# Split queries and keys copied from their tile to the matmul stacks in 18 SBUF transfers per unit, without the scratch tensor in DRAM

## The reference

```
g = (x * ac_w + ac_b) * x;  g = clip(g, 0, 6)                 # x is _gn(x)
qkv = einsum('bchw,dc->bdhw', g, qkv_w)                       # split into q, k, v: 16 heads x 8 channels
attn = softmax(einsum('wnqd,wnkd->wnqk', q, k) * scale)       # inside each 8x8 window
out = einsum('bchw,dc->bdhw', einsum('wnqk,wnkd->wnqd', attn, v), proj_w) + proj_b
x = x + L0(_gn(x))
x = x + conv3x3(_gn(x), W) + bias
```

## Time and profile before

| what | value |
|---|---|
| median of three runs | 1202.87 us |
| the profiled execution | 1207.08 us, of it a span of 1205.3 us |
| TensorE matmul busy | 1015.8 us (84%) |
| VectorE busy | 983.1 us (82%) |
| ScalarE busy | 791.3 us (66%) |
| GpSimd busy | 503.8 us (42%) |
| mean granted TensorE clock | 0.947 |
| DMA packets, bytes | 114917, 140.59 MB |

### The profile page before, as it was taken

One profiled execution on the slowest core, in us unless ns is written; L12 is line 12 of the kernel. 1 busy time (PEld: TensorE's weight loads), 2 busy tenths in 40 slices (PEclk: granted clock), 3 DMA queues, 4 the chain that ended last, 5 costly groups with the idle time before them and its releaser, 6 DMA issues.

```text
span 1205.3 us, 52690 instructions
## 1 busy us (share of the span) xinstructions
PE 1015.8 (84%) x23011; PEld 582.6 (48%) x23011; DVE 983.1 (82%) x1312; ACT 791.3 (66%) x1327; POOL 503.8 (42%) x469
## 2 busy tenths in 40 slices
PE   0388999999999985998853899999999999779996
PEld 0155565556555652433321555556655655334442
DVE  6786888889888754899986788888988976379996
ACT  1257787778778774655532688878887877556663
POOL 5214454445444433233343245545454544404335
PEclk9879999999999997999986899999999999879998
DMA  8234444444444420133343454444444444001112
GB/s 307 84 118 125 136 138 138 136 137 128 135 142 135 142 64 1 44 129 108 105 157 122 123 150 139 136 137 138 144 132 148 134 142 126 4 1 53 70 70 88
DMA packets 114917, 140.59 MB, mean 117 GB/s; under 512 B 25088, under 2 KB 91008, under 8 KB 113664
## 3 DMA queue, kind: packets, MB, share of 16 engines
q1 hardware_dynamic: 114688, 137.23, 36.3%
HBM read 67.96 MB, written 67.11 MB: 112 GB/s over the span
## 4 chain that ended last, share of the span: by engine, by line
PE 63%; DVE 18%; issue 8%; DMA 4%; ACT 3%; SPq 2%; POOL 2%; POOLq 0%; DVEq 0%; ACTq 0%
PE ps L918 11%; PE ps L899 11%; PE ps L926 9%; PE ps L885 8%; PE ps L995 6%; PE ps L853 5%; DVE work L760 5%; PE ps L854 5%; PE ps L855 5%; DVE work L756 4%; PE ps L872 4%; DVE st L610 1%; SPq L288 1%; DVE work L738 1%; DMA q_bd<-stack_scratch 1%
## 5 line engine op out<-in xcount | busy, mean ns | idle before, releaser
L654 DVE TENSOR_REDUCE m_all<-ps 128x16 f32<-128x1024 f32 x256 | 313.5, 1225 | 114.9 <-PE ps L885 114.3
L370 POOL TENSOR_SCALAR work<-work 128x256 f32<-128x256 f32 x128 | 108.6, 849 | 401.2 <-DVE work L647 352.4
L885 PEld LDWEIGHTS ps<-k_pl,q_bd 48*64 48x64 f16 x8192 | 90.4, 111 | 174.5 <-issue 126.9
L448 ACT ACTIVATE late_probs<-ps,ws 128x1024 f32<-128x1024 f32 x128 | 142.8, 1116 | 44.6 <-PE ps L899 42.8
L853 PE MATMUL ps<-work,c_hi 128*128 128x512 f16 x384 | 148.3, 386 | 27.7 <-DVE work L760 27.7
L899 PE MATMUL ps<-q_bd,k_pl 128*64 128x256 f16 x2048 | 163.8, 282 | 7.5 <-ACT work L448 4.0
L885 PE MATMUL ps<-k_pl,q_bd 48*64 48x64 f16 x8192 | 118.6, 198 | 57.3 <-issue 39.4
L536 ACT CAST work<-work 128x512 f16<-128x512 f32 (+1 forms) x128 | 79.0, 622 | 115.8 <-DVE work L756 107.9
L448 ACT ACTIVATE work<-ps,ws 128x1024 f32<-128x1024 f32 x128 | 141.7, 1107 | 13.1 <-PE ps L899 11.5
L854 PE MATMUL ps<-work,c_lo 128*128 128x512 f16 x384 | 148.0, 385 | 0.0
L855 PE MATMUL ps<-work,c_hi 128*128 128x512 f16 x384 | 147.4, 384 | 0.0
(11 more groups left out here) (126 smaller groups left out, 1894.1 us busy)
## 6 DMA issues: line engine op xcount, KB each, us to landing
stack_scratch<-work SPq DMA_DIRECT2D x128, 256.0 KB, 2.4
q_bd<-stack_scratch SPq DMA_DIRECT2D x256, 96.0 KB
k_pl<-stack_scratch SPq DMA_DIRECT2D x128, 192.0 KB, 3.5
stack_scratch<-work SPq DMA_DIRECT2D x128, 128.0 KB, 2.5
out_dram<-work SPq DMA_DIRECT2D x32, 512.0 KB, 2.9
img<-in_x_dram SPq DMA_DIRECT2D x8, 1024.0 KB, 13.4
img<-in_x_dram SPq DMA_DIRECT2D x16, 512.0 KB, 4.3
q_bd<-m_pair SPq DMA_DIRECT2D x256, 8.0 KB
```

The source lines that it names most:

```text
L370: g.tensor_scalar(near[h], near[h], -2.0, None, ALU.add).then_inc(less_done, 1)
L448: a.activation(probs[h][:, p % 2, :], ps[:, ST_B:ST_B + 2, :].rearrange("p w t -> p (w t)"), ACT.Exp, scale=ws[:, R_EXP:R_EXP + 1]).then_i ...
L654: v.tensor_reduce(m_all[:, 0, :, p], ps[:, S_B:S_B + 2, :].rearrange("p r (a k) -> p (r a) k", k=WIN), AX.X, ALU.max).then_inc(max_done, 1)
L885: mm = t_.matmul(ps[64 * w:64 * w + 64, S_B + r, at:at + WIN], q_bd[rows, md, r, g, j, tok], k_pl[rows, md, g, tok], start=True, stop=True)
```

## The change

The scratch tensor in DRAM, `write`, `q_sent` and `k_sent` go. SyncE copies each part of `qk` straight to every third partition of the stacks: for the keys 3 parts times 2 halves, 6 transfers of 64 rows of 1 KB; for the queries 3 parts times 4 quarters, 12 transfers of 32 rows of 1 KB. Keys now go before queries, and the maxima stand ahead of both. ScalarE's next rounding of `qk` waits until the transfers have landed in the stacks (`k_in`, `q_in`) where it waited for the write to DRAM (`k_sent`, `q_sent`). So that a part's rows are neighbours in `qk`, the columns of the query and key weights are put in another order once, at the start: three copies where there was one, on ScalarE and on VectorE.

```diff
-        q_sent = sem("q_sent", 32); k_sent = sem("k_sent", 32)
-        q_in = sem("q_in", 64); k_in = sem("k_in", 32)
+        q_in = sem("q_in", 16 * HR * HJ * PARTS); k_in = sem("k_in", 16 * HR * PARTS)
...
                 def queries_in(d, md):
-                    after(sp, q_sent, d)
+                    after(sp, q_lo_done, d)
                     after(sp, st_done, d - BUFS)
                     after(sp, q_in, d - 1)
-                    q_rows = stackd[md, 0].rearrange("(r g j d) s t -> r j (d s) g t", r=HR, g=HG, j=HJ)
-                    for r in range(HR):
-                        for j in range(HJ):
-                            at = 64 * r + HROWS * j
-                            sp.dma_start(q_bd[at:at + HROWS, md, r, :, j, :], q_rows[r, j]).then_inc(q_in, 16)
+                    for s, part in enumerate((0, 1, 1)):
+                        for r in range(HR):
+                            for j in range(HJ):
+                                at, ch = 64 * r + HROWS * j, 64 * r + 32 * j
+                                sp.dma_start(q_bd[at + s:at + HROWS:PARTS, md, r, :, j, :], qk[ch:ch + 32, part, :]).then_inc(q_in, 16)
 
                 def keys_in(d, md):
-                    after(sp, k_sent, d)
+                    after(sp, k_lo_done, d)
                     after(sp, st_done, d - BUFS)
                     after(sp, k_in, d - 1)
-                    k_rows = stackd[md, 1].rearrange("(r g a) s t -> r (a s) g t", r=HR, g=HG)
-                    for r in range(HR):
-                        sp.dma_start(k_pl[64 * r:64 * r + ROWS, md, :, :], k_rows[r]).then_inc(k_in, 16)
+                    for s, part in enumerate((2, 3, 2)):
+                        for r in range(HR):
+                            sp.dma_start(k_pl[64 * r + s:64 * r + ROWS:PARTS, md, :, :], qk[64 * r:64 * r + 64, part, :]).then_inc(k_in, 16)
...
+                    if live(1):
+                        maxima(n + 1, (m + 1) % BUFS)
                     if live(3):
+                        keys_in(n + 3, (m + 3) % BUFS)
                         queries_in(n + 3, (m + 3) % BUFS)
-                        keys_in(n + 3, (m + 3) % BUFS)
-                    if live(2):
-                        maxima(n + 2, (m + 2) % BUFS)
-                    if live(4):
-                        after(sp, q_in, n + 1)
-                        write(0, n + 4, (m + 4) % BUFS, q_lo_done, q_sent)
-                        after(sp, k_in, n + 1)
-                        write(1, n + 4, (m + 4) % BUFS, k_lo_done, k_sent)
...
-            a.copy(w_hi[:, :, :], ps[:, 0, 0:3 * P].rearrange("p (t d) -> p t d", t=3)).then_inc(act_step, 1)
+            for k in range(3):
+                a.copy(by_column(w_hi, k), by_head(k)).then_inc(act_step, 1)
...
                         after(act, k_done, n + 3)
-                        after(act, k_sent, n + 2)
+                        after(act, k_in, n + 2)
                         a.copy(qk[:, 2, :], ps[:, GB, :]).then_inc(k_hi_done, 1)
...
                         after(act, q_done, n + 3)
-                        after(act, q_sent, n + 2)
+                        after(act, q_in, n + 2)
                         a.copy(qk[:, 1, :], ps[:, GA, :]).then_inc(q_hi_done, 1)
```

More of the change, by code:

```diff
@@ L61, in build @@
 def build(nc, x, ac_w, ac_b, qkv_w, proj_w, proj_b, conv_w, conv_b, out):
-    stackd = nc.dram_tensor("stack_scratch", [BUFS, 2, P, PARTS, UT], F16, kind="Internal").ap()
     ctx = ExitStack()
@@ L188, in pixels, with by_head, by_column @@
             return (u // ACROSS) * WS, (u % ACROSS) * UCOL
+        def by_head(k):
+            cols = ps[:, 0, k * P:k * P + P]
+            return cols if k == 2 else cols.rearrange("p (r g j d) -> p r j d g", r=HR, g=HG, j=HJ)
+        def by_column(w, k):
+            return w[:, k, :] if k == 2 else w[:, k, :].rearrange("p (r j d g) -> p r j d g", r=HR, j=HJ, g=HG)
         block = ctx.enter_context(nc.Block())
@@ L599, in weak_weights @@
                 for j in range(MATS // 4):
-                    dve.wait_ge(act_step, 3 + j)
+                    dve.wait_ge(act_step, 5 + j)
                     v.tensor_tensor(c_lo[:, 4 * j:4 * j + 4, :], ps[:, 2 + j, :].rearrange("p (t d) -> p t d", d=P),
@@ L606, in _ @@
                 if i == 2:
-                    dve.wait_ge(act_step, 1)
-                    link(v.tensor_tensor(w_lo[:, :, :], ps[:, 0, 0:3 * P].rearrange("p (t d) -> p t d", d=P), w_hi[:, :, :], ALU.subtract))
+                    dve.wait_ge(act_step, 3)
+                    for k in range(3):
+                        link(v.tensor_tensor(by_column(w_lo, k), by_head(k), by_column(w_hi, k), ALU.subtract))
                 dve.wait_ge(x_in[i * LOADS // UNITS], 16)
@@ L855, in three @@
                 return t_.matmul(o, lhs_hi, rhs_lo, start=False, stop=last)
-            pe.wait_ge(act_step, 2)
+            pe.wait_ge(act_step, 4)
             norm_mean(0)
```

## The result

The changed kernel takes 1541.93 us (median of four runs, 1540.04 to 1554.21), the kernel before 1201.18 beside it: a ratio of 1.285, 95% interval 1.276 to 1.294. It is slower, as forecast, but by 341 us where 210 were forecast: 1542 against 1413, just inside the upper edge of the range (1280 to 1545), next to the 1545 of the rival "heavier than that".

What follows compares the result with a forecast made beforehand. TensorE bounds the kernel at 12.0 us a unit; the new ring takes 9.5 issues + 1.7 stalls + 1.7 landing + 2.5 rest = 15.4, with starts 105 us per image, 210 in all: 1413 us, range 1280 to 1545.

Steps and rivals of the forecast that it cites:

- heavier than that: Rival, chance 0.17: all eighteen issues at 0.635 us, TensorE's clock lower, lap (a unit's period) 17.7 us, total 1545.
- What bounds the kernel now: Attention loop runs at TensorE's pace, 12.0 us a unit; SyncE's queue has thin cover, some landings late.
- The ring: SyncE's transfers, landing, ScalarE's rounding and exponential, TensorE, st_done, next keys: one lap 15.4 us against 12.0.
- The price of a query issue: Each SyncE query transfer holds the queue 0.53 us; the step trusted least, 0.1 us being 95 us in all.
- The two ends: Issue prices taken as limits: 0.615 us for SyncE's maxima transfers, 0.40 for its reads from DRAM.
- The key issue: Each of six 64-row key transfers on SyncE priced at the upper end, 0.615 us.
- Landing and way back: After the last query issue: 1.7 us to land, 2.5 through ScalarE and TensorE until the next keys.
- Stalls: SyncE's queue at times held longer for the same work: 1.7 us per 18 issues.
- How many laps, and the start: 28 longer laps per image, 95 us, plus 10 us together for the stage's start and last units.
- Bytes and weights: Halved DMA traffic costed at nothing; extra weight copies on ScalarE at the start cost nothing.
- Cheap issues: Rival, chance 0.12: SyncE's transfers cost 0.40 us like reads, lap 12.3 us, 27 us more, total 1230.
- the faster side: Rival, chance 0.04: an issue costs 0.33 us or less, TensorE binds at 11.2, late landings go, total 1155.

Runs made afterwards that it cites:

- e8: Kernel before with three DRAM writes a unit instead of four, second copies of queries and keys merged into one transfer: 1221.70 us (1.010).
- e6: Kernel before with SyncE's four writes to DRAM put ahead of the maxima transfers: 1317.20 us (1.093).
- e12: Changed kernel with two qk tiles, TensorE's last transposed scores ahead of the waiting scores, and ten transfers (keys, third query part) on GpSimd: 1170.88 us (0.973).
- e2: Changed kernel with two qk tiles in turn, so ScalarE's rounding waits for the landing of the unit before the last: 1471.01 us (1.221).
- e3: Changed kernel with two qk tiles, and TensorE's last part of the transposed scores ahead of the scores that wait for transfers: 1468.43 us (1.218).
- e1_price: Kernel before with eleven bursts of 12 transfers, one shape each, after its last output; only issue times read: new forms 0.713 and 0.637 us.
- e5_short_rows: Changed kernel with all 18 transfers a unit but each row cut from 1 KB to 128 bytes: 1527.71 us (1.263).
- e9_pool_keys: Changed kernel with two qk tiles, TensorE's last transposed scores ahead of the waiting scores, and keys issued by GpSimd at its iteration's end: 1548.97 us (1.280).

## Why the prediction was right, and where it was short

**What bounds the kernel now: right.** TensorE set the pace of the kernel before (93% and 94% busy), and the transfers had little slack: `e8` shows a time 12 us longer when the tiles' way waits 0.9 us more a unit, and `e6` shows that the maxima beside them had 2 to 3 us. That the way of the tiles itself cost time before fits `e12` (a mean lap of 11.4 us against 12.2 in the first image, while TensorE's waits for these landings fell from 24.0 to 8.2 us over both images), but no run changes that alone.

**The ring: right, and seen whole.** Landing, rounding and exponential, last part of the transposed scores, `st_done`, keys: each handover stands in the rows of after, and the maxima are hidden (SyncE waits from 302.60 to 304.23, 1.6 us; 1.2 forecast). `e2` and `e3` add that the queue itself comes next, 22 issues and 15.2 us, only 1.5 us under the ring. The prediction gave the ring's ties and its issues as one sum; the experiments part them: with both ties cut, 74 of the 341 us come back, and the other 267 stay with the length of the queue.

**The price of a query issue: the term most undersized.** It was put at 0.53 us, between the maxima's 0.615 and the reads' 0.40, because the transfer fills whole rows of partitions as the reads do. It costs 0.713, above both ends. From first query issue to last that is 7.94 against 5.83 us, 2.1 us a lap. The two ends were not bounds. The prediction put the gap between maxima and reads down to the two sides' shapes and then took off 0.085 for full rows. What parts the two rows is that both sides lie in SBUF: at 32 rows on both sides an issue still costs 0.633 (`e1_price`), and bytes do not count (`e5_short_rows`). The last 0.08, from 0.633 to 0.713, goes with 8 destination partitions (L335 and L344 of `e1_price`); why they cost more stays open. The key issue, 0.615 forecast, costs 0.636.

**Landing and way back: 0.3 us short each.** 2.07 for 1.75, and 2.79 for 2.45, the latter because L898 took 1.07 us at a granted clock of 0.56 where 0.63 was the row at full clock. The effect was named only in the heavy rival.

**Stalls: 1.3 us too long.** The mean lap from the maxima is 17.1 us, 0.4 over the undisturbed 16.69, where 1.7 was forecast from two units of before. So the lap: 15.4 + 2.1 + 0.2 + 0.3 + 0.3 - 1.3 = 17.0.

**How many laps, and the start: short.** The period holds for all 30 units from the second on, (610.7 - 95.2 - 1.9) / 30 = 17.1 and (1366.6 - 854.2 - 1.9) / 30 = 17.0:

```profile
L290 SPq DMA_DIRECT2D q_bd<-m_pair x124: 503/586/1777, 95.2 to 610.7; - x124
...
L290 SPq DMA_DIRECT2D q_bd<-m_pair x124: 502/586/1189, 854.2 to 1366.6; - x124
```

The forecast had 28 laps and 10 us of start per image; the second unit's maxima come 95.2 - 80.1 = 15.1 us later. 2 x (30 x 5.1 + 15) = 336, the 333 us between the two spans. First scores begin at 63.24 where 62 was forecast.

**Bytes and weights: right.** Halved traffic is worth nothing by itself, and the weight copies cost nothing: VectorE's statistics end at 34.1 us in the profile after.

**The prediction's own sums.** Three do not come out as written, none of them large. The lower end of the range, 1280, is called an issue of 0.45; by its own 95 us for each 0.1 us that is about 1310, and 1280 belongs to an issue of 0.42. The first scores add up to 51.1 + 10.0 + 1.7 = 62.8, not 62. And the maxima's bytes move 1.15 to 1.33 us after the issue starts, not 1.2 to 1.4.

**Luck.** The mechanism was right, but the central sum was 131 us short of 341. It lay inside the range only because the upper end was drawn at the heavy rival's 1545, 3 us above the result, and that rival's terms were off in both directions: its issues too short (10.8 us a lap against 3.89 + 7.94 = 11.8), its laps too few (28 against 30), its stalls too long (2.2 against 0.4).

**The rivals.** Cheap issues and the faster side are out by the price. Behind the latter stood the Trainium skill's rule that the issue time is usually small relative to the DMA itself ("DMA: Bandwidth & Descriptors", "Issuing engines are not separate DMA queues"). It does not hold here: the eighteen issues hold the queue 12.4 us a unit, the last lands 2 us after it starts, and ten issues moved to GpSimd are worth 298 us (1468.43 to 1170.88). The heavy rival had the right total for partly the wrong reasons.

## What to carry to other kernels

- Count DMA instructions per iteration and engine queue, at the price of each form, before counting bytes; 22 issues of 0.6 to 0.7 us are a lap of 15 us though the DMA engines are 85% idle.
- When a copy loses its middle buffer, look at what the middle buffer untied: here the source tile came free only after the last hop, and destination reuse, scores and the next rounding closed a ring. Give the tile a second buffer first, then share the issues between queues.
- Before placing transfers in another engine's program, look at how far ahead it runs: GpSimd, an iteration ahead, stood 7.5 us a unit for keys that were not made yet, and the same six instructions were worth 1549 us in one place and 1214 in the other.

## What was not expected of the hardware

- A DMA instruction on SyncE holds its queue 0.58 to 0.77 us when both sides are in SBUF and 0.30 to 0.43 us when one is in DRAM (rows neighbouring). Bytes hardly count: 0.584 at 4 KB, 0.601 at 128 KB, and in one form 0.671 at 4 KB and at 32 KB. SBUF to SBUF, 8 and 24 partitions (0.625 to 0.672 and 0.714 to 0.772) cost more than 4, 16, 32, 64 or 128 (0.584 to 0.601). One read from DRAM with a step of three rows cost 0.655.
- The same 64-row transfer holds GpSimd 0.51 us and SyncE 0.59. Here, that made GpSimd a good second queue.
- Longer issues go with instruction loading: every issue of an attention unit over 0.9 us overlaps a 16 KB packet of the instruction queue in time, 105 of 105 in the kernel before and 47 of 47 after (counted in the packets of the two traces); but 152 of the 791 and 313 of the 1361 shorter issues overlap one too, so a packet does not always stall, and that it is the cause is not shown. None of GpSimd's 384 key issues in `e9_pool_keys` was long, though 82 overlapped such a packet. Why the changed kernel, which issues more, has fewer long ones was not found.
